# Local attention weights laid out by quadrant, and worked through the engines quadrant by quadrant

## What is computed

```
xn = _layernorm(x)
# branch 1: local attention, 16 query heads of 32, 4 key/value heads, window of 64 keys back
q, k, v = xn @ Wq.T + bq, xn @ Wk.T + bk, xn @ Wv.T + bv
q, k = rope(rmsnorm(q)), rope(rmsnorm(k))
scores = einsum('bhqd,bhkd->bhqk', q, k) * scale
scores = where((q_index < k_index) | (abs(q_index - k_index) > 64), -10000, scores)
out1 = einsum('bhqk,bhkd->bhqd', softmax(scores), v).reshape(B, S, 512) @ Wo.T + bo
# branch 2: causal attention over all keys; one key and one value of 32 per token,
# chosen among 16 heads by the largest gate
gating = softmax(xn @ W_gate.T)
k_shared, v_shared = chosen key, chosen value * gate
out2 = softmax(causal(q2 @ k_shared / sqrt(32))) @ v_shared
return x + out1 + out2
```

## Time and profile before

| | us |
|---|---|
| median of 3 runs | 685.91 |
| lowest and highest | 684.29, 686.01 |
| span of the profiled execution | 684.4 |
| TensorE busy | 646.0 |
| VectorE busy | 496.3 |
| GpSimd busy | 442.6 |
| ScalarE busy | 362.5 |

### The profile page before, as it was taken

The page is one execution under the profiler, slowest core; times in us unless marked ns, Lnnn a source line. Parts: engine busy times, 40 slices in busy tenths (PEclk is TensorE's granted clock), DMA queues, the critical chain, the costliest instruction groups (busy, mean ns, idle before and its releaser), DMA issues.

```text
span 684.4 us, 19451 instructions
## 1 busy us (share of the span) xinstructions
PE 646.0 (94%) x7432; PEld 510.2 (75%) x7432; DVE 496.3 (73%) x1328; ACT 362.5 (53%) x906; POOL 442.6 (65%) x368
## 2 busy tenths in 40 slices
PE   3788999999999899999899899999999999999997
PEld 3577888887788688888688667777777777777775
DVE  3956966677678866787676368888888787879454
ACT  4436444472527344445335555556566566656674
POOL 3965764938195735684487267685868777778730
PEclk9979999999999999999999999999999999999999
DMA  8522213231232032222214541321314131402011
GB/s 295 206 59 86 82 38 115 86 98 51 66 102 61 30 112 70 64 70 74 77 32 118 158 142 56 96 64 50 111 49 110 51 106 32 110 28 87 4 33 33
DMA packets 64942, 56.61 MB, mean 83 GB/s; under 512 B 6481, under 2 KB 48849, under 8 KB 64849
## 3 DMA queue, kind: packets, MB, share of 16 engines
q1 hardware_dynamic: 62704, 54.45, 27.2%
q10 hardware_dynamic: 2144, 0.93, 0.5%
HBM read 37.20 MB, written 17.89 MB: 80 GB/s over the span
## 4 chain that ended last, share of the span: by engine, by line
PE 78%; DVE 9%; POOL 4%; ACT 3%; issue 2%; DMA 2%; ACTq 1%; DVEq 0%; POOLq 0%
PE gemm L938 17%; PE s_ps L1047 12%; PE od_ps L1096 11%; PE st_ps L1080 10%; PE gemm L1024 6%; PE od_ps L1110 5%; PE win L998 3%; PE gemm L934 3%; PE win L983 2%; PE s_ps L1119 2%; DMA rope_t<-rope 2%; PE av L1010 2%; DVE l_sum L1266 2%; ACT p_loc L1492 2%; DVE l_max L1257 1%
## 5 line engine op out<-in xcount | busy, mean ns | idle before, releaser
L938 PE MATMUL gemm<-w_tok,xt 128*128 128x512 f32 (+1 forms) x768 | 186.1, 384 | 3.3 <-DVE x_res L1283 0.9
L938 PEld LDWEIGHTS gemm<-w_tok,xt 128*128 128x128 f32 x768 | 131.7, 193 | 28.2 <-issue 1.4
L1318 DVE CUSTOM_DVE_ANT_0 s_ps<-s_ps,x_ln 128x512 f32<-128x512 f32 (+3 forms) x224 | 127.6, 620 | 24.4 <-PE s_ps L1047 24.0
L1047 PE MATMUL s_ps<-k_stack,w_tok 96*128 96x512 f32 (+2 forms) x336 | 101.5, 385 | 0.3 <-DVE x_res L1283 0.3
L1080 PE MATMUL st_ps<-w_tok,k_stack 98*128 98x512 f32 x288 | 99.0, 413 | 0.2 <-ACT p_loc L1540 0.2
L1540 ACT ACTIVATE p_loc<-st_ps 128x512 f32<-128x512 f32 x144 | 77.7, 599 | 36.0 <-PE st_ps L1080 34.8
L1634 POOL TENSOR_TENSOR rope_b<-qkv,sin_t 128x128 f32<-128x128 f32 (+1 forms) x32 | 27.5, 880 | 79.5 <-DVE qkv L1232 79.3
L1047 PEld LDWEIGHTS s_ps<-k_stack,w_tok 96*128 96x128 f32 x336 | 55.0, 188 | 28.3 <-DVE picked_fk L1318 12.4
L1492 ACT ACTIVATE p_loc<-win,l_max 128x96 f32<-128x96 f32 x256 | 60.9, 391 | 19.1 <-DVE l_max L1257 19.0
L934 PE MATMUL gemm<-xt,w_qt 128*128 128x256 f32 x384 | 57.1, 293 | 6.3 <-DVE picked_fv L1211 3.5
L1540 ACT ACTIVATE p_loc_t<-st_ps 128x512 f32<-128x512 f32 x96 | 52.4, 599 | 19.8 <-PE st_ps L1080 19.3
(11 more groups left out here) (172 smaller groups left out, 1298.7 us busy)
## 6 DMA issues: line engine op xcount, KB each, us to landing
w_tok<-q_parts SPq DMA_DIRECT2D x72, 128.0 KB, 2.6
q_parts<-qt SPq DMA_DIRECT2D x120, 64.0 KB
x_ln<-x SPq DMA_DIRECT2D x8, 512.0 KB, 4.7
x_res<-x SPq DMA_DIRECT2D x16, 256.0 KB, 2.9
partial<-x_res SPq DMA_DIRECT2D x16, 256.0 KB, 2.6
w_tok<-partial SPq DMA_DIRECT2D x8, 512.0 KB, 5.2
raw<-w_tok SPq DMA_DIRECT2D x3, 1024.0 KB, 12.9
v_win<-v_rows SPq DMA_DIRECT2D x64, 48.0 KB, 2.2
```

The source lines that it names most:

```text
L938: i = e.matmul(g[:, 0:cols], xs[l][:, k, a * P:(a + 1) * P], w_tok_p[r][:, k, c0:c0 + cols], start=first, stop=last)
L1047: e.matmul(s_ps[bank][:, 0:cols], q_op[b][0:HALVES, i, h, :], k_stack[0:HALVES, b * S + c0:b * S + c0 + cols], start=True, stop=True).then ...
L1318: e.tensor_tensor_reduce(out=s[:, 0:cols], in0=s[:, 0:cols], in1=causal[:, S - width + c0:S - width + c0 + cols], scale=1.0, scalar=dst if ...
```

## The change

`p_loc` is laid out by quadrant first and key head second. `weights`, `sums` and `scaled` become steps of one quadrant each: four exponentials, a reduction of 384 columns with a reciprocal of 4, and a product over 384 columns. Each has its own mark, so that a quadrant's `sums` wait for its own exponentials, its `scaled` for its own reciprocals, and its `p_t` for its own `scaled`. `l_max`, `l_sum` and `l_rec` are ordered by quadrant too. In the plan a tile starts four chains `quadrant`; the banks of `win` still come free only when the last quadrant's exponentials end. `res_bias` goes with the last quadrant. Two small things beside it: the last two `qt` steps wait in the plan until the last rotation has been issued, and `max_low` of unit 0 is issued together with `max_in_rows`.

```diff
         do("maxima", m, a)
         yield 0, [("V", 1.75)]
-        do("weights", m, a)
-        def exps_end(end):
-            win_free[:] = [end - 1.1 * (HKV - 1 - g) + HOP for g in range(HKV)]
-        yield 0, [("A", 4.4)], exps_end
-        do("sums", m, a)
-        yield 0, [("V", 2.0)]
-        do("scaled", m, a)
-        do("res_bias", m, a)
-        yield 0, [("G", 2.9)], lambda end: p.busy(end, ("G", 1.3))
-        yield 0, [("", SLACK)]
+        turned = []
         for quad in range(QUADS):
-            while not win_ready(quad):
-                yield None
-            win_free[quad] = None
-            p.take(("win", quad), ("p_t", m, a, quad), ("p_t_r", (m, a, quad)))
-            do("p_t", m, a, quad)
-            yield 0.45, []
-            win_free[quad] = p.busy(p.now, ("A", 0.6)) + HOP
+            p.add(quadrant(m, a, quad, turned))
+        while len(turned) < QUADS:
+            yield None
...
+    def quadrant(m, a, quad, turned):
+        do("weights", m, a, quad)
+        yield 0, [("A", 1.2)], lambda end: quad < QUADS - 1 or win_free.__setitem__(slice(None), [end + HOP] * HKV)
+        do("sums", m, a, quad)
+        yield 0, [("V", 0.6)]
+        do("scaled", m, a, quad)
+        if quad == QUADS - 1:
+            do("res_bias", m, a)
+        yield 0, [("G", 0.75), ("", SLACK)], lambda end: quad == QUADS - 1 and p.busy(end, ("G", 1.3))
+        while not win_ready(quad) or len(turned) < quad:
+            yield None
+        win_free[quad] = None
+        p.take(("win", quad), ("p_t", m, a, quad), ("p_t_r", (m, a, quad)))
+        do("p_t", m, a, quad)
+        turned.append(quad)
+        yield 0.45, []
+        win_free[quad] = p.busy(p.now, ("A", 0.6)) + HOP
...
     def take_qt(n, kind, c, freed):
+        while (n, c) in LAST_CHUNKS and not p.roped:
+            yield None
         do("qt", n, c)
...
-    p_loc = [sb(one, f"p_loc{a}", [P, HKV, QUADS, KEYS]) for a in range(2)]
+    p_loc = [sb(one, f"p_loc{a}", [P, QUADS, HKV, KEYS]) for a in range(2)]
...
             elif step == "sums":
-                e.tensor_reduce(l_sum[:, a, :], p_loc[a][:, :, :, :].rearrange("p g s k -> p (g s) k"), AX.X,
-                                ALU.add).then_inc(*M["l_sum"].did((m, a)))
+                part = slice(quad * HKV, (quad + 1) * HKV)
+                lane.wait_ge(*M["p_exp"].of((m, a, quad)))
+                e.tensor_reduce(l_sum[:, a, part], p_loc[a][:, quad, :, :], AX.X, ALU.add).then_inc(
+                    *M["l_sum"].did((m, a, quad)))
...
             elif step == "weights":
                 for g in range(HKV):
-                    for quad in range(QUADS):
-                        n = g * QUADS + quad
-                        i = e.activation(p_loc[a][:, g, quad, :], win[:, g, quad * KEYS:(quad + 1) * KEYS], ACT.Exp,
-                                         bias=l_max[:, a, n:n + 1])
-                    i.then_inc(*M["p_exp"].did((m, a, g)))
+                    n = quad * HKV + g
+                    i = e.activation(p_loc[a][:, quad, g, :], win[:, g, quad * KEYS:(quad + 1) * KEYS], ACT.Exp,
+                                     bias=l_max[:, a, n:n + 1])
+                i.then_inc(*M["p_exp"].did((m, a, quad)))
...
             elif step == "scaled":
+                p_l = p_loc[a][:, quad, :, :]
+                lane.wait_ge(*M["l_rec"].of((m, a, quad)))
+                e.tensor_tensor(p_l, p_l, l_rec[:, a, quad * HKV:(quad + 1) * HKV].unsqueeze(2).to_broadcast(
+                    [P, HKV, KEYS]), ALU.mult).then_inc(*M["p_r"].did((m, a, quad)))
```

35 lines of the change are left out of this document (15 added, 20 removed).

## The result

The changed kernel takes 692.22 us (median of four runs, 689.86 to 693.53) against 685.96 (684.29 to 687.57) for the kernel before on the same chip: a ratio of 1.009, 95% interval 1.0064 to 1.0115. The forecast was 686.8, with a range up to 691.5; the likeliest case was taken as +0.9 us, +6.3 were measured, and the time lies 0.7 us outside.

What follows compares the result with a forecast made beforehand. TensorE was taken as the bound, busy 646.0 of a 684.4 us span. Start +0.8, `fk_lo` −2.0, new waits +2.0 and drain +0.1 summed to +0.9: a median of 686.8 us, eight-in-ten range 681.5 to 691.5.

Steps and rivals of the forecast that it cites:

- Prices: Per quadrant piece: sum 0.54 us plus reciprocal 0.18 on VectorE, scaling 0.84 on GpSimd; +0.9 and +0.6 us a tile.
- The start: Start of the overlapped stage: first sums piece and reciprocal delay `picked_fv` of tile (0, 1); +0.8 us, ends +0.3 and +1.5.
- `fk_lo`: Overlapped stage: shorter GpSimd scalings cut this VectorE step's stalls to at most 0.84 us each; −2.0 us, ends 0 and −3.3.
- The new waits: Overlapped stage: transposes closer behind their scores, and pieces ahead of bank releases, make TensorE wait; +2.0 us, ends 0 and +6.2.
- slower by queueing on VectorE: Rival: sums pieces with reciprocals (0.78 us) queue ahead of reads that free product banks, TensorE waits; +4.4, 690.3 us; chance 0.35.
- the drain: End of the last tile: values 1.4 us earlier, lower clock takes back 1.5; +0.1 us in all.
- The banks: Each `win` bank holds all four quadrants' scores, so no transpose may write its bank before the last exponential.
- the walk: Last tile followed step by step: scores start at 380.25 us, values at 392.3 against 393.71 before, −1.4 us.
- The clock term: Last tile's end: half granted clock would lie over values and projection; +1.5 us, bounds 0 and +4.1.

Runs made afterwards that it cites:

- late-bank order: Kernel before, its planner told that all four `win` banks come free together when a tile's exponentials end; whole sums and scaling: 685.89 us, ratio 1.0002.
- nearly free pieces: Changed kernel in its own order, each sums piece adding only 8 of its 96 keys: 686.64 us, ratio 0.9999.
- the run with the last tile alone by head group: Kernel before with only the last tile's sums and scaling split in four, one piece per head group, layout and exponentials kept: 684.78 us, ratio 0.9998.

## Why the prediction was wrong

**Prices: right.** Sums pieces 0.541 us (0.54), scalings 0.827 (0.84). The cadence of a piece with its reciprocal is 0.67, less than the 0.78 forecast: they run back to back without a hop.

**The start: a miss.** +0.8 forecast, 0 measured. `picked_fv` of the second tile ran at 54.56 and TensorE waited 0.57 us for it, less than the 1.29 of the earlier trace rows: the planner had moved what stands around it too.

**`fk_lo`: the size right, the reason in part.** −2.0 forecast, −3.0 measured. VectorE's longest `fk_stack` instruction is now 1.13 us where it was 2.29. It does not lie beside a scaling, though, but beside another GpSimd product, and ends 0.05 us after it:

```profile
335.60 1.27 POOL L1625 TENSOR_TENSOR qkv<-qkv,rms_y 128x640 f32<-128x640 f32 x1
335.79 1.13 DVE L1230 TENSOR_TENSOR fk_stack<-chosen_fk,fk_stack 128x32 fp32r<-128x32 f32 x1
```

So "such a stall is at most 0.84" was wrong: the scaling is not the only product that stretches it. The page "SBUF — State Buffer", section "Who interferes with whom", of the Trainium skill says that a VectorE instruction with two SBUF inputs contends with a GpSimd instruction that reads SBUF, for a port pair that is locked exclusively; the two rows agree. Nor is the fall of the waits the pieces' work alone: with whole scalings in the late-bank order they are 0.5 us too, while four pieces in a row ahead of `fk_lo` made one of 1.68 us in the order of before.

**The new waits: this step failed.** "I take +2.0", with ends of 0 and 6.2. Measured are 9.2, above the term's own upper end, or 6.2 net of `fk_lo`. Two errors lie in it.

First, the size: I took a third of the upper bound "since VectorE is busy for 228.5 of 312 us only and can mostly catch up". An average share says nothing of that. The waits with a piece ahead rose by up to 4.9 us, and nearly free pieces take 4.7 us of waits out of the changed kernel. One site of the late-bank order shows the full 0.70 us of the pieces passed on. The rival *slower by queueing on VectorE*, at 690.3, named this mechanism; part of it is what happened.

Second, the kind: the term priced only the pieces' own neighbourhoods and took the rest of the order as no worse than before. But 4.6 us of new waits have no piece ahead of them: those for the attention add ahead of `first_max` (0 to 2.3), for ScalarE's copies `q_t` and `k_t` (0.5 to 1.3), and the 1.70 us for `picked_fk` at 259.89. They stay when the pieces are nearly free; I put them down to the new places of other steps. Orders with no piece at all lost 5 to 10 us in three of four cases, in waits and in clock. The upper end should have held that cost, and the lower end of 0 was not near. From the trace of before it could not be read, but the order of the changed kernel, laid beside the old one, showed that much had been placed anew, and that alone was reason for a wider upper end.

**The range: too narrow by its own terms.** The written sum for the upper end, +5.8, gives 691.7 and not 691.5. It also takes `fk_lo` and the drain at their likeliest values (−2.0 and +0.1), not at their upper ends (0 and +2.7); with these it would have been 696.3.

**The banks: seen by half.** The text said that no transpose may enter before the last exponential, of the same tile. That it stops the *previous* tile's transposes is what forces a new order. In itself it costs nothing once planned for (685.9 us).

**The drain: the walk was right, the clock was not.** Scores to values 11.6 us against 12.05 forecast. The clock term of +1.5 was wrong here: the granted clock stayed at 1.00. In the run with the last tile alone by head group it came as described, with 1.5 us on the projection.

**What stays open.** How much of the 6.3 us is the split and how much the luck of its order can't be settled from these runs: in the order of before the same pieces (by head group) changed nothing measurable (−1.4 us), in another they cost 9.2. The profiled execution, 688.6 us of span, is the shortest of the four. Their spans go to 692.3 and their mean granted clocks from 0.991 down to 0.989, which can account for some 1.4 of the 3.7 us (an estimate, 0.002 of the span); no trace of a longer one was taken. The undisturbed test, whole sums in the exact order of the changed kernel, wasn't tried, and neither were the two small edits alone (the `qt` steps that wait for the rotation, and `max_low`), which move the order too.
